# A graph layer on one core: the root ahead of the weights, minima behind the node tiles, zeros shared with ScalarE, and another order of VectorE's last steps

## The chip, the cores and the metric

The kernel runs on one core of a Trainium2 chip. The metric is the device time of one execution, in microseconds (us). Engines are named TensorE (PE in rows), VectorE (DVE), ScalarE (ACT), GpSimd (POOL) and SyncE (SP). They run side by side and wait for one another by semaphores.

## The reference

One layer of a message-passing network over 3125 nodes of 160 numbers (64 scalars and 32 vectors of 3) and 53125 edges, sorted by their destination.

```python
h = maximum(layernorm(x), 0)
s, v = h[:, :64], h[:, 64:].reshape(n, 32, 3)
xs = s @ W1_s / 8;  xv = einsum('nmc,mk->nkc', v, W1_v) / sqrt(32)
w = silu(edge_embed @ fc_w1 + fc_b1) @ fc_w2 + fc_b2          # 192 weights for each edge
xs_e, xv_e = xs[src], xv[src]                                  # gathered rows
msg = [w_ss*xs_e*sh0, w_vv*sum_c(xv_e*sh1)/sqrt(3), w_sv*xs_e (x) sh1, w_vs*xv_e*sh0]
agg = segment_sum(msg, dst, n) / sqrt(0.5)
out_s = agg_s @ W2_s / sqrt(96) + s @ Wsc_s / 8                # and the same for out_v
out = x + h + [silu(out_s[:, :64]), out_v * silu(out_s[:, 64:96])]
```

## The kernel before

**Node stage.** The nodes are 25 tiles of 125, in 5 groups of 5. For each group VectorE takes statistics (L291) and aggregates them to mean and variance (L296), ScalarE takes the root (`std`, L258), VectorE the reciprocal (L302) and the product -mean x scale (`nmr`, L303), and then writes the five normalised tiles (L309). TensorE transposes each tile (L413, L414). ScalarE applies the maximum while it copies the result to `hT` (L245). TensorE multiplies it with the weights (L428, L429), two tiles behind the transposes, and ScalarE copies the products of two tiles at a time to `prod` (L250). SyncE stores them to `table` in HBM, in five parts of 6, 6, 6, 4 and 3 tiles (L200). A root is issued by ScalarE behind the third tile of the group before it: `if t % G == 2`. The first root stands behind the scalings of the weights (L237, L239), which wait for their loads.

Beside this, work for the edge stage is done. VectorE's `minima` (eight instructions on 104 partitions, L317 to L327) finds the lowest destination of each tile of 128 edges. It stands behind group 1. TensorE's multiplication L419 spreads the minima over the partitions ahead of the products of tile 18, and `windows` (L355) takes the destinations relative to them. The accumulator `agg`, 12548 columns, is cleared: 8192 columns by four transfers of 2048 from a tile of zeros (L193), the other 4356 by ScalarE behind the last products (L253). ScalarE fills `emb` with zeros at the start (L234). GpSimd gathers 24 "raw" tiles, input rows instead of table rows (L220). VectorE takes moments of two of the four groups of 6 raw tiles here (`raw_moments`), the rest in the edge stage.

**Barrier.** The node stage is a block of its own. All engines meet at its end, then each reads the number of passes (L493). There is one pass here.

**Edge stage.** The 416 tiles of 128 edges are 104 steps of 4 tiles, numbered q from 0. In each, GpSimd gathers the rows of the sources (L535), one instruction per tile. Every fourth step from 11 on has a raw tile as its last, which TensorE multiplies itself, so that 392 gathers are left. A slot for gathered rows is free when VectorE has multiplied the step four earlier. TensorE makes the edge weights (L811, L824), VectorE multiplies them with the rows (`products`: L640 and twice L645), TensorE sums over edges by selectors (`scatter`: L829, L830, L834), and VectorE adds the sums into `agg` at 4 windows (`add_windows`: L625 and L631, which make the selectors of a step two later, and four times L683). Step q of VectorE's program does the additions of step q - 2 first, and then the products of step q. Nodes whose edges are all in leave beside: ScalarE copies their sums (L550), TensorE multiplies them (L859 to L866), ScalarE applies silu (L560, L561), VectorE multiplies by the gates (`gated`, L702), adds the input (`with_input` L695, `residual` L708), and SyncE stores the tile.

**The end.** The last step, 103, goes tile by tile: `last_products(j)` (L657, L661), `last_scatter(j)`, `last_add(j)` (L690). Its first three tiles are gathered, the fourth is the raw one. TensorE's order at the end is the weights of step 103, the sums of step 102, its own part of the last node tile, the last scatters 0 and 1, node tile 23, the last scatters 2 and 3, and the sums of node tile 24.

## Time and profile before

| | us |
|---|---|
| median of 3 runs | 546.01 (545.75 to 546.27) |
| the profiled execution | 545.95 |
| its span | 544.3 |
| GpSimd busy | 397.7 (73%) |
| TensorE busy | 475.8 (87%) |
| VectorE busy | 354.1 (65%) |
| ScalarE busy | 202.1 (37%) |
| mean granted TensorE clock | 0.936 of full |

The page divides the span by what ended last. 65% of that chain is the gathers of L535 and 22% is "issue", time in which an engine waited for nothing that the profile shows. TensorE's 87% includes the modelled ends of pipelined matmuls, so it is not an engine at its peak. A row of the timeline gives the start, the duration, the engine, the line and the operation, what it writes and reads, how many are merged in it, and in brackets the idle time ahead of it with what ended it.

### The profile page before, as it was taken

Reading aid. Unit: us, or ns where it says so; the run is one execution under the profiler, and the core shown is the slowest. Engines: PE = TensorE matmul, PEld = TensorE weight load, DVE = VectorE, ACT = ScalarE, POOL = GpSimd, SP = SyncE. Lnnn points to the kernel's source line nnn. Section 1 sums busy time; section 2 is a strip of 40 time slices with the busy share of each in tenths; the row PEclk is TensorE's granted clock in tenths of the full one; section 3 lists DMA queues with packets and bytes.
Section 4 is the critical chain, followed back from the end, with each engine's and each line's share of the span. In section 5 each row is a group of like instructions: output and inputs, shape, how many; then the busy total and the mean of one; then the engine's idle time right before and its main releaser. Section 6 shows DMA issues by size and latency. Waiting matters only on the chain.

```text
span 544.3 us, 16081 instructions
## 1 busy us (share of the span) xinstructions
PE 475.8 (87%) x5423; PEld 354.8 (65%) x5423; DVE 354.1 (65%) x1234; ACT 202.1 (37%) x412; POOL 397.7 (73%) x429
## 2 busy tenths in 40 slices
PE   6848779899898998999898999899898998998995
PEld 6745556667665765767575676567575765765675
DVE  7865565665676676567656766675576677676754
ACT  4564422343343333343333434343333334243331
POOL 7737777777777777777777777777777777777770
PEclk9888798899899899899997999899899899998996
DMA  9982222223222222222222222222222222222221
GB/s 223 395 265 72 70 71 71 67 66 81 77 76 67 76 73 69 74 77 76 65 73 77 66 77 77 76 65 74 77 76 67 77 77 69 72 75 75 66 75 30
DMA packets 35375, 48.06 MB, mean 88 GB/s; under 512 B 9749, under 2 KB 27956, under 8 KB 34844
## 3 DMA queue, kind: packets, MB, share of 16 engines
q0 software_dynamic: 19968, 34.11, 23.2%
q1 hardware_dynamic: 14977, 13.65, 8.4%
q8 instruction: 9, 0.15, 0.1%
q10 hardware_dynamic: 410, 0.07, 0.1%
q14 instruction: 11, 0.08, 0.0%
HBM read 39.60 MB, written 4.00 MB: 80 GB/s over the span
## 4 chain that ended last, share of the span: by engine, by line
POOL 65%; issue 22%; PE 4%; DVE 4%; DMA 3%; ACT 0%; ACTq 0%; DVEq 0%; SPq 0%
POOL gath L535 65%; DMA table<-prod 1%; DMA gath<-table,src_sb 1%; DMA w_v_in<-wscv 1%; PE ps L428 1%; PE ps L429 1%; DVE stats L291 1%; DVE z_sb L309 1%; DVE P L645 1%; PE ps L824 0%; PE ps L413 0%; PE ps L834 0%; PE ps L866 0%; PE ps L414 0%; ACTq L230 0%
## 5 line engine op out<-in xcount | busy, mean ns | idle before, releaser
L535 POOL DMA_INDIRECT gath<-table,src_sb x392 | 371.6, 948 | 125.9 <-issue 118.8
L834 PE MATMUL ps<-S,P 128*64 128x24 f32 x2496 | 170.7, 220 | 0.0
L824 PE MATMUL ps<-fc_sb,hid 128*128 128x384 f32 x416 | 164.9, 522 | 0.0
L829 PE MATMUL ps<-S,P 128*64 128x36 f32 x832 | 119.2, 237 | 49.3 <-DVE agg L683 48.3
L834 PEld LDWEIGHTS ps<-S,P 128*64 128x64 f32 x2496 | 159.5, 142 | 0.0
L829 PEld LDWEIGHTS ps<-S,P 128*64 128x64 f32 x832 | 82.3, 139 | 113.5 <-DVE agg L683 72.6
L640 DVE TENSOR_TENSOR P<-ps,gath 128x512 f32<-128x512 f32 x103 | 71.2, 692 | 125.5 <-PE ps L824 63.7
L568 ACT ACTIVATE hid<-ps,fb_sb 128x256 f32<-128x256 f32 x104 | 49.2, 473 | 185.7 <-PE ps L811 128.8
L830 PE MATMUL ps<-S,P 128*64 128x12 f32 x832 | 108.9, 209 | 0.0
L645 DVE TENSOR_TENSOR P<-ps,gath 128x384 f32<-128x384 f32 x206 | 104.3, 548 | 0.0
L824 PEld LDWEIGHTS ps<-fc_sb,hid 128*128 128x128 f32 x416 | 81.3, 206 | 34.4 <-issue 6.7
L683 DVE TENSOR_TENSOR agg<-ps,agg 128x48 f32 x412 | 84.5, 205 | 27.4 <-DVE agg L683 0.3
L583 ACT COPY ps<-fb_sb 128x768 f32<-128x768 f32 x104 | 83.9, 806 | 8.7 <-DVE P L645 8.5
L830 PEld LDWEIGHTS ps<-S,P 128*64 128x64 f32 x832 | 84.4, 142 | 0.0
L811 PE MATMUL ps<-emb,fc_sb 128*128 128x256 f32 x208 | 76.2, 449 | 0.0
L550 ACT COPY aggT<-agg 128x500 f32 (+1 forms) x24 | 26.9, 1119 | 40.4 <-DVE agg L683 40.4
L631 DVE TENSOR_TENSOR S<-M,sh_sb 128x192 f32<-128x192 f32 x104 | 37.3, 358 | 0.9
L560 ACT ACTIVATE gates<-ps 125x32 f32<-125x32 f32 x25 | 4.9, 197 | 84.1 <-PE ps L866 78.4
L811 PEld LDWEIGHTS ps<-emb,fc_sb 128*128 128x128 f32 x208 | 33.0, 198 | 4.2 <-issue 1.2
L625 DVE TENSOR_TENSOR M<-iota,dstrel 128x48 f32<-128x48 f32 x104 | 21.6, 208 | 15.6 <-issue 8.1
L220 POOL DMA_INDIRECT raw<-x,src_sb x24 | 22.8, 952 | 7.2 <-issue 7.2
L866 PE MATMUL ps<-wo_v,aggT 96*125 96x32 f32 x144 | 18.4, 264 | 0.0
(118 smaller groups left out, 351.9 us busy)
## 6 DMA issues: line engine op xcount, KB each, us to landing
gath<-table,src_sb POOLq DMA_INDIRECT x392, 2.5
agg<-zeros SPq DMA_DIRECT2D x4, 1024.0 KB, 16.9
out<-res SPq DMA_DIRECT2D x24, 78.1 KB
x_sb<-x SPq DMA_DIRECT2D x5, 350.0 KB
emb<-emb_t SPq DMA_DIRECT2D x104, 16.0 KB
table<-prod SPq DMA_DIRECT2D x3, 420.0 KB
sh_sb<-sh_t SPq DMA_DIRECT2D x1, 840.0 KB
raw<-x,src_sb POOLq DMA_INDIRECT x24, 7.3
```

The source lines that it names most:

```text
L535: nc.gpsimd.indirect_dma_start(gath[:, u, j, :], None, table, bass.IndirectOffsetOnAxis(ap=src_sb[:, t:t + 1], axis=0)).then_inc(arrived, 16)
L568: ins = nc.scalar.activation(hid[:, u % 2, :, :].rearrange("p g e -> p (g e)"), hid_ps, ACT.Silu, bias=fb1_sb[:, 0:1])
L583: nc.scalar.copy(w_ps(u)[:, :, 0:WN], fb2_sb[:, :].unsqueeze(1).broadcast_to([128, QT, WN])).then_inc(p_seed, 1)
L631: nc.vector.tensor_tensor(S[:, u % 2, :, :, :], M[:, :, :].unsqueeze(3).broadcast_to([128, QT, WIN, 4]), sh_sb[:, bass.ds(q * QT, QT), :]. ...
L640: nc.vector.tensor_tensor(pu[:, :, 0:128].rearrange("p j (a m) -> p j a m", a=2), w[:, :, 0:128].rearrange("p j (a m) -> p j a m", a=2), g ...
L645: ins = nc.vector.tensor_tensor(pu[:, :, 128:PC].rearrange("p j (c a m) -> p j c a m", c=NC, a=2)[:, :, :, a, :], w[:, :, lo:lo + V0].unsq ...
L683: nc.vector.tensor_tensor(a, out_ps(q)[:, j, :, :].rearrange("p n c -> p (n c)"), a, ALU.add).then_inc(p_agg, 1)
L811: ins = nc.tensor.matmul(hid_ps, fc1_sb[:, :], emb[:, u, :], start=True, stop=True)
L824: ins = nc.tensor.matmul(w_ps(u)[:, 2 * g:2 * g + 2, 0:WN], hid[:, u % 2, g, :], fc2_sb[:, :, :], start=False, stop=True, skip_group_check ...
L829: nc.tensor.matmul(oj[0:64, :, 0:3], pj[:, 64:128], sj[:, :, 1:4], start=True, stop=True)
L830: nc.tensor.matmul(oj[0:64, :, 3], pj[:, 0:64], sj[:, :, 0], start=True, stop=True)
L834: ins = nc.tensor.matmul(oj[64:128, :, c:4:3 - c], pj[:, lo:lo + 64], sj[:, :, 0:2 + c:1 + c], start=(c == 0), stop=(c == NC - 1), skip_gr ...
```

## The change

In the node stage:

- The first root is issued ahead of the scalings of the weights (`table_weights`).
- The product `nmr` goes. The tiles are normalised as (x - mean) x scale instead of x x scale + nmr.
- `minima` and the multiplication for it stand behind all the tiles.
- Two transfers of zeros are left. ScalarE clears four parts of 1024 columns behind tiles 2, 6, 11 and 16, and 4356 columns behind the last products as before. The fill of `emb` stands behind that.
- One raw group of four is taken in the node stage, and three in the edge stage.

At the end:

- VectorE adds the sums of step 101, and takes the inputs of the last two tiles, ahead of the products of step 102.
- The raw tile of step 103 is multiplied and summed first, and the first of the last additions stands between the products.
- The residual of node tile 22 stands behind the last additions.

```diff
-ZEROS, ZERO_DMA = 2048, 8192
+ZEROS, ZERO_DMA, ZERO_PART = 2048, 4096, 1024
+CLEARS = (2, 6, 11, 16)
-HEAD_RAW = 2
+HEAD_RAW = 1
 (ScalarE)
-                nc.scalar.copy(emb[:, :, :], zero[:, 0:1].unsqueeze(2).broadcast_to([128, SLOTS, 2 * TE]))
...
                 std(0)
+                table_weights()
                 for t in range(NN):
                     h_columns(t)
+                    if t in CLEARS:
+                        lo = ZERO_DMA + ZERO_PART * CLEARS.index(t)
+                        clear(lo, lo + ZERO_PART)
                     if t % G == 2 and t // G + 1 < NG:
                         std(t // G + 1)
...
-                clear(ZERO_DMA, (N + WIN) * AC)
+                clear(ZERO_DMA + ZERO_PART * len(CLEARS), (N + WIN) * AC)
+                nc.scalar.copy(emb[:, :, :], zero[:, 0:1].unsqueeze(2).broadcast_to([128, SLOTS, 2 * TE])).then_inc(s_cact, 1)
 (VectorE)
-                    link(nc.vector.reciprocal(rstd[:, sl], rstd[:, sl]))
-                    nc.vector.scalar_tensor_tensor(nmr[:, sl], meanvar[:, sl, 0], -1.0, rstd[:, sl],
-                                                   ALU.mult, ALU.mult).then_inc(s_rstd, 1)
+                    nc.vector.reciprocal(rstd[:, sl], rstd[:, sl]).then_inc(s_rstd, 1)
...
-                        nc.vector.tensor_scalar(z_sb[:, t, :], x_sb[:, t, :], rstd[:, t:t + 1], nmr[:, t:t + 1],
-                                                ALU.mult, ALU.add).then_inc(s_z, 1)
+                        nc.vector.tensor_scalar(z_sb[:, t, :], x_sb[:, t, :], meanvar[:, t, 0:1], rstd[:, t:t + 1],
+                                                ALU.subtract, ALU.mult).then_inc(s_z, 1)
...
-                    if g == 1:
-                        minima()
-                raw_moments(0)
+                minima()
+                for g in range(HEAD_RAW):
+                    raw_moments(g)
                 windows()
-                raw_moments(1)
 (VectorE, edge stage)
                     def step(i, u, tile=None):
                         q = i * SLOTS + u
+                        if isinstance(i, int) and q == NQ - 1:
+                            return last(tile)
...
+                        if isinstance(i, int) and q == NQ - 2:
+                            cols = columns(q - 1)
+                            add_windows(q - 1, u + 1, cols)
+                            with_input(NN - 2)
+                            with_input(NN - 1)
                         products(i, q, u)
...
                     def last(tile):
-                        residual(tile)
+                        last_products(QT - 1)
                         last_products(0)
-                        with_input(NN - 2)
-                        last_products(1)
-                        with_input(NN - 1)
                         cols, rest = columns(NQ - 2), columns(NQ - 1)
                         dve.wait_ge(n_cols, NN - 1)
                         add_windows(NQ - 2, SLOTS - 2, cols, more=False)
+                        last_products(1)
+                        last_add(0, rest[QT - 1])
                         last_products(2)
-                        last_products(3)
-                        for j in range(QT):
-                            last_add(j, rest[j])
+                        for k in range(1, QT):
+                            last_add(k, rest[k - 1])
+                        residual(tile)
```

`last_scatter` and `last_ps` count in the new order (k), and the tile that k stands for is (3 + k) mod 4.

On ScalarE, at the start of the node stage, these rows stand in the kernel before:

```order
L232 ACTIVATE root<-eps 125x1
L234 COPY emb<-zero 128x1024
L237 ACTIVATE w_s<-w_s 64x160
L239 ACTIVATE w_tab<-w_v_in,own_c 96x32 x3
L258 ACTIVATE rstd<-meanvar,eps 125x5
L245 ACTIVATE hT<-ps 96x250 x3
L258 ACTIVATE rstd<-meanvar,eps 125x5
```

And these in the changed one:

```order
L232 ACTIVATE root<-eps 125x1
L259 ACTIVATE rstd<-meanvar,eps 125x5
L238 ACTIVATE w_s<-w_s 64x160
L240 ACTIVATE w_tab<-w_v_in,own_c 96x32 x3
L246 ACTIVATE hT<-ps 96x250 x3
L254 COPY agg<-zero 128x1024
L259 ACTIVATE rstd<-meanvar,eps 125x5
```

The first root moved ahead of the scalings, the fill of `emb` left this place, and a clear of `agg` stands between the third tile and the next root.

On VectorE, at the end of the edge stage, from the products of step 102 on, the kernel before has:

```order
L640 TENSOR_TENSOR P<-ps,gath 128x4x128
L645 TENSOR_TENSOR P<-ps,gath 128x4x3x32 x2
L702 TENSOR_TENSOR res<-ps,gates 125x3x32
L668 TENSOR_LOAD base_i
L625 TENSOR_TENSOR M<-iota,dstrel 128x48
L683 ISA
L683 TENSOR_TENSOR agg<-ps,agg 128x48
L631 TENSOR_TENSOR S<-M,sh_sb 128x192
```

The changed kernel has, from the third addition of step 101's sums on (`ISA` is a wait):

```order
L685 ISA
L685 TENSOR_TENSOR agg<-ps,agg 128x48
L685 ISA
L685 TENSOR_TENSOR agg<-ps,agg 128x48
L697 SCALAR_TENSOR_TENSOR xh<-z_sb,x_sb 125x160 x2
L642 TENSOR_TENSOR P<-ps,gath 128x4x128
L647 TENSOR_TENSOR P<-ps,gath 128x4x3x32 x2
L704 TENSOR_TENSOR res<-ps,gates 125x3x32
L659 TENSOR_TENSOR P<-ps,gath 128x128
L663 TENSOR_TENSOR P<-ps,gath 128x192
```

The additions of step 101 and the two inputs moved from behind the products of step 102 to ahead of them, and the raw tile's products follow at once.

## Rows read from the trace of the kernel before

**Rows 1.** The page's groups of instructions: busy and mean | idle before.
```profile
L535 POOL DMA_INDIRECT gath<-table,src_sb x392 | 371.6, 948 | 125.9 <-issue 118.8
```

**Rows 2.** Timeline of GpSimd in the edge stage: first and last gather.
```profile
40.89 0.96 POOL L535 DMA_INDIRECT gath<-table,src_sb  x1 [6.79 <-DMA table<-prod]
...
530.62 0.95 POOL L535 DMA_INDIRECT gath<-table,src_sb  x1 [0.30 <-issue]
```

**Rows 3.** The chain of waits, 0 to 42 us: start, length, what.
```profile
28.38 0.70 PE ps L419 x2
...
33.05 0.30 ACT prod L250
...
35.16 5.08 DMA table<-prod
```

**Rows 4.** Timeline of VectorE, node stage and the first instruction behind it.
```profile
7.23 0.44 DVE L296 BATCH_NORM_AGGREGATE meanvar<-stats 125x2 f32<-125x6 f32 x5
8.57 0.17 DVE L303 SCALAR_TENSOR_TENSOR nmr<-meanvar,rstd 125x5 f32<-125x5 f32 x1
13.47 1.51 DVE L309 TENSOR_SCALAR z_sb<-x_sb,rstd,nmr 125x160 f32<-125x160 f32 x5
15.26 0.65 DVE L317 TENSOR_REDUCE dmax<-dq 104x4 f32<-104x512 int32 x1
...
17.78 1.22 DVE L291 BATCH_NORM_STATS2 stats<-x_sb 125x6 f32<-125x160 f32 x5
...
27.44 1.73 DVE L309 TENSOR_SCALAR z_sb<-x_sb,rstd,nmr 125x160 f32<-125x160 f32 x5
...
37.59 0.13 DVE L350 COPY raw_mean<-raw_mv 128x6 f32<-128x6 f32 x1
40.37 0.38 DVE L614 TENSOR_SCALAR dstrel<-dstrel 128x416 f32<-128x416 f32 x1 [2.66 <-PEq L180]
```

**Rows 5.** Timeline of ScalarE, node stage.
```profile
4.73 1.03 ACT L234 COPY emb<-zero 128x1024 f32<-128x1024 f32 x1
...
8.03 0.29 ACT L258 ACTIVATE rstd<-meanvar,eps 125x5 f32<-125x5 f32 x1
...
15.92 0.29 ACT L258 ACTIVATE rstd<-meanvar,eps 125x5 f32<-125x5 f32 x1
...
33.23 3.82 ACT L253 COPY agg<-zero 128x4356 f32<-128x4356 f32 x1
```

**Rows 6.** Timeline of TensorE: the first transpose of two tiles in succession.
```profile
29.36 0.27 PE L413 MATMUL ps<-ident,z_sb 125*64 125x125 f32 x1
...
30.01 0.27 PE L413 MATMUL ps<-ident,z_sb 125*64 125x125 f32 x1
```

**Rows 7.** Timeline of GpSimd, its last instruction in the node stage.
```profile
33.16 0.95 POOL L220 DMA_INDIRECT raw<-x,src_sb  x1 [0.30 <-issue]
```

**Rows 8.** Three stretches: busy us (instructions) by engine, granted clock, DMA share, GB/s.
```profile
17.20:20.62 3.42, 1.03 (x10) 0.88 (x9) 3.34 (x14) 0.93 (x3) 2.54 (x3) 1.00 1.01 394
20.62:24.04 3.42, 3.42 (x19) 3.30 (x18) 3.03 (x17) 1.73 (x5) 2.77 (x3) 0.50 1.02 393
...
36.00:38.00 2.00, 0.00 (x0) 0.00 (x0) 0.43 (x4) 1.45 (x3) 0.00 (x0) 0.92 1.04 292
```

**Rows 9.** Timeline of VectorE, the end.
```profile
529.37 0.69 DVE L640 TENSOR_TENSOR P<-ps,gath 128x512 f32<-128x512 f32 x1 [1.72 <-DMA gath<-table,src_sb]
...
531.07 0.20 DVE L625 TENSOR_TENSOR M<-iota,dstrel 128x48 f32<-128x48 f32 x1
...
537.31 0.21 DVE L690 TENSOR_TENSOR agg<-ps,agg 128x48 f32 x1 [0.20 <-PE ps L834]
```

**Rows 10.** Timeline of TensorE, the end.
```profile
528.83 0.51 PE L834 MATMUL ps<-S,P 128*64 128x24 f32 x6
...
531.04 0.25 PE L829 MATMUL ps<-S,P 128*64 128x36 f32 x1 [0.21 <-DVE P L645]
...
536.64 0.49 PE L834 MATMUL ps<-S,P 128*64 128x24 f32 x3
```

More of the change, by code:

```diff
@@ L33 @@
 EPS = 1e-5
-ZEROS, ZERO_DMA = 2048, 8192
+ZEROS, ZERO_DMA, ZERO_PART = 2048, 4096, 1024
 WARM_NODES = 17
-MINB_AT = 20
 PC = 320
@@ L124, in build @@
         rstd = sbt("rstd", [NTN, NN])
-        nmr = sbt("nmr", [NTN, NN])
         w_v_in = sbt("w_v_in", [VD, 2, V0])
@@ L232, in _, with table_weights @@
                 nc.scalar.activation(root[:, :], eps[0:NTN, :], ACT.Sqrt)
-                nc.scalar.copy(emb[:, :, :], zero[:, 0:1].unsqueeze(2).broadcast_to([128, SLOTS, 2 * TE]))
-                act.wait_ge(s_own, 2)
-                act.wait_ge(s_wn, 16 * len(node_loads))
-                nc.scalar.activation(w_s[0:S0, :], w_s[0:S0, :], ACT.Copy, scale=S0 ** -0.5)
-                for comp in range(NC):
-                    ins = nc.scalar.activation(w_tab[:, V0 * comp:V0 * (comp + 1)], w_v_in[:, 0, :], ACT.Copy,
-                                               scale=own_c[:, comp:comp + 1])
-                ins.then_inc(s_scaled, 1)
+                def table_weights():
+                    act.wait_ge(s_own, 2)
+                    act.wait_ge(s_wn, 16 * len(node_loads))
+                    nc.scalar.activation(w_s[0:S0, :], w_s[0:S0, :], ACT.Copy, scale=S0 ** -0.5)
+                    for comp in range(NC):
+                        ins = nc.scalar.activation(w_tab[:, V0 * comp:V0 * (comp + 1)], w_v_in[:, 0, :], ACT.Copy,
+                                                   scale=own_c[:, comp:comp + 1])
+                    ins.then_inc(s_scaled, 1)
                 def h_columns(t):
@@ L297, in mean_and_variance, with scale @@
                     ins.then_inc(s_stat, 1)
-                def scale_and_bias(g):
+                def scale(g):
                     sl = slice(g * G, g * G + G)
                     dve.wait_ge(s_std, g + 1)
-                    link(nc.vector.reciprocal(rstd[:, sl], rstd[:, sl]))
-                    nc.vector.scalar_tensor_tensor(nmr[:, sl], meanvar[:, sl, 0], -1.0, rstd[:, sl],
-                                                   ALU.mult, ALU.mult).then_inc(s_rstd, 1)
+                    nc.vector.reciprocal(rstd[:, sl], rstd[:, sl]).then_inc(s_rstd, 1)
                     dve.wait_ge(s_rstd, g + 1)
@@ L379, in _ @@
                 mean_and_variance(0)
-                scale_and_bias(0)
+                scale(0)
                 normalised(0)
@@ L386, in _ @@
                         tile_stats(g + 1)
-                    scale_and_bias(g)
+                    scale(g)
                     normalised(g)
@@ L415, in _ @@
                                             ident[0:NTN, 0:NTN]).then_inc(s_hT, 1)
-                    if t == MINB_AT:
-                        pe.wait_ge(s_ones, 1)
-                        pe.wait_ge(s_mm, 1)
-                        nc.tensor.matmul(minb_ps, ones[:, :], diag.rearrange("p q t -> p (q t)"),
-                                         start=True, stop=True).then_inc(s_minb, 1)
                     if t >= 2:
@@ L430, in _ @@
                                          start=True, stop=True).then_inc(s_prod, 1)
+                pe.wait_ge(s_ones, 1)
+                pe.wait_ge(s_mm, 1)
+                nc.tensor.matmul(minb_ps, ones[:, :], diag.rearrange("p q t -> p (q t)"),
+                                 start=True, stop=True).then_inc(s_minb, 1)
                 nc.tensor.transpose(most_ps, most[:, :], ident[0:NQ, 0:NQ]).then_inc(s_row, 1)
@@ L746, in step @@
                             add_windows(q - 2, u, cols)
-                        if isinstance(i, int) and q == NQ - 1:
-                            return last(tile)
+                        if isinstance(i, int) and q == NQ - 2:
[3 more added lines that the diff above has]
+                            with_input(NN - 1)
                         products(i, q, u)
```

28 lines of the change are left out of this document (14 added, 14 removed).

## The prediction, made before the changed kernel ran

> **What bounds the kernel now.** I read the page's groups first, then GpSimd's timeline, then the chain of waits. The 392 gathers of the edge stage are GpSimd's, and their group shows 125.9 us of idle time, of which 118.8 is its own issue gap [rows 1]. That leaves 7.1 us of true waiting, and 6.79 of it is the one wait ahead of the first gather [rows 2]. So from 40.89 to 530.62 us GpSimd never waits for TensorE, VectorE or ScalarE, and nothing in that stretch can be shortened by other engines. The profiled time of 544.3 us of span (545.95 with what lies around it, 0.06 under the median of 546.01) is three pieces: 40.89 until the first gather starts, 489.7 of gathers, and 13.7 from the start of the last gather to the end. The change touches the first and the last. It leaves the number of gathers alone.
>
> The first gather has two things ahead of it, and they are nearly tied. The chain goes by the last store of the table: last copy of products until 33.35 (33.05 + 0.30), its second store issued 35.16, landed 40.24 (5.08 later), gather 0.65 after that [rows 2, 3]. But VectorE ends the node stage at 37.72 (37.59 + 0.13), and its first instruction of the edge stage starts at 40.37, having waited for the barrier [rows 4]. I read the 0.65 us behind the landing, where 0.30 is the usual gap, as a sign that GpSimd too came through that barrier late. So both must get earlier, and I keep the distance from VectorE's end to the first gather, 40.89 - 37.72 = 3.17 us.
>
> **The node stage, part by part.** Call X the end of the last copy of products by ScalarE: 33.35 now.
>
> Root first, no second operand. The first group's moments end at 7.67 on VectorE (7.23 + 0.44) [rows 4], the root starts at 8.03, because four scalings of weights stand ahead of it [rows 5]. Behind the change it can start at 7.69: 0.34 gained. The scalings move behind it and end near 8.95, before the first transposed tile needs ScalarE. The product of mean and scale goes, an instruction of 0.17 and its gap, 0.20 per group [rows 4]. With two groups of it, normalising of group 1 starts at 13.47 - 0.34 - 0.40 = 12.73. The normalisation itself keeps its form and length.
>
> Minima behind the tiles. They hold VectorE from 15.26 to 17.78, 2.52 us [rows 4], and TensorE starves meanwhile. What is late next? Not VectorE: a group without minima and product takes it 3.1 us (statistics 1.1, being the 1.22 of the row less the overlap with the next, reciprocal 0.2, five tiles 1.45, aggregation 0.35). Not TensorE, at 0.65 per tile (29.36 to 30.01) or 3.3 per group [rows 6]. It is ScalarE, since the root of group g+2 stands behind the third tile of group g+1. Today from the start of group 1's normalisation (13.47) to the root at 15.92 are 2.45 us [rows 4, 5]. Each of the four clears of 1024 columns is the same operation as the fill of emb, 1.03 us [rows 5], of which I count 0.95 (the next one overlaps its end). 0.22 of it falls into a wait of ScalarE for TensorE, so the root comes 2.45 + 0.73 = 3.18 after the tiles start, and the next tiles 0.54 later (root 0.32, reciprocal 0.22): a period of 3.72 us. Three periods from 12.73: group 4 starts at 23.9, against 27.44 now.
>
> From there to X are 33.35 - 27.44 = 5.91 us today, with the multiplication for the minima, 0.70, in the middle, which goes behind [rows 3, 4]. So X = 23.9 + 5.91 - 0.70 = 29.1, 4.25 earlier. Bounds of this: TensorE's 3.3 per group instead of 3.72 gives X = 27.8; all of each clear on the path (3.95 per group) and 1.9 more for a stretch at the low clock gives X = 31.7.
>
> Behind X. The clear of 4356 columns stays, 3.82 [rows 5]. New between it and the root for the raw tiles is the fill of emb, +0.95; one root and one pair of VectorE instructions go, -0.19. VectorE now ends 37.72 - 33.35 = 4.37 after X, then 5.13 after X: 34.2. VectorE's own work does not end it: tiles done at 25.5, minima 2.5, moments 1.9, windows 1.0, rest 1.2, near 32.1. GpSimd does nearly: its raw gathers, untouched, end at 34.11 (33.16 + 0.95) [rows 7]. First gather: 34.2 + 3.17 = 37.4, **3.5 us earlier**. GpSimd's 34.11 is the floor, so no more than 3.6 can come of it, and with X = 31.7 it is 0.9.
>
> Zeros. The transfers run at a DMA share of about 1 until 38 us [rows 8], which is what makes the last store take 5.08. Two of the four 1 MB transfers go. At the 394 GB/s of the row at 17.20 their 2.1 MB (twice 128 x 2048 x 4 bytes) are 5.3 us of queue, so the last store lands near 35, ahead of the 36.9 at which VectorE passes the barrier (34.2 + 40.37 - 37.72). I cost it at nothing because ScalarE's clears cover it. If that were wrong, see the fourth rival.
>
> Raw groups. One more group of moments (6 statistics, 6 aggregations, 1.9 us) falls into the edge stage's first steps. GpSimd is released by VectorE's products four steps ahead and never waited, so: 0.
>
> **The tail.** Now, in VectorE's order: step 102 of 0 to 103 multiplies at 529.37, when the gather lands, after 1.72 us of waiting [rows 9]. The addition of step 101's sums follows at 531.07 and ends at 532.37, then the inputs of two tiles, 0.5 us. After the change these 1.8 us stand ahead of the multiplication. The idea needs step 101's sums to be ready while VectorE waits. They are not: TensorE ends them at 529.34 (528.83 + 0.51) [rows 10], the very moment the gather lands. So the additions start at 529.5, end at 530.8, inputs until 531.3, and the multiplication starts 1.9 us late. TensorE is what waits for it: its scatter of step 102 starts at 531.04 now [rows 10], at 532.95 then. From 531.04 to the end of the last scatter, 537.13, are 6.1 us [rows 10], of which I read 0.3 as waits for VectorE and 0.5 as the low clock; the other 5.3 (scatter 1.5, own part 0.5, two last scatters 0.8, node tile 1.4, two last scatters 1.1) are TensorE's own and end at 538.2. The last addition can start 0.15 later, 538.4, against 537.31 now [rows 9]: +1.1. If the last two scatters run at 1.2 GHz, as their like does now from 536.04 on, +1.5. I take **+1.3**. Raw tile first and the additions laid between are worth nothing by themselves, because TensorE is the later one. The residual moved behind the additions falls into VectorE's wait for the last tile's gates: 0, and its store still leaves ahead of the last tile's. Bounds: 0 (if a scatter ends earlier than this trace shows) to +2.9 (second rival).
>
> Sum: -3.5 + 1.3 = -2.2, from 546.0 to 543.8 us.
>
> **Clock.** While the minima hold VectorE, in the stretch from 17.20 to 20.62, TensorE was busy 1.03 of 3.42 us, and the next stretch was granted 0.50, 1.2 GHz [rows 8]. The minima made that gap, so I expect the node stage to keep 2.4 GHz. The tail gets a new gap, 530.8 to 532.95. The Trainium skill, "TensorE: Matmul & The Clock Gate", section "Part 1: The HAM clock gate", says that the clock follows how busy TensorE has been recently and that the observation runs free of the program. By that rule the node stage wins and the tail can lose; the trace agrees on the first place. It gives the second rival a chance, and the sum stays as it is without it.
>
> **Rivals.**
> 1. Forecast, 543.8, own range 542.9 to 544.9: 58%.
> 2. The new gap brings the tail to 1.2 GHz three microseconds earlier. Six tile scatters then cost 0.45 instead of 0.35 each, own part and node tile about 1 us more together: +1.6 to the tail, 545.4. For: [rows 8]. Against: the gap is 2.1 us, and that stretch had 2.4 idle. 17%.
> 3. No loss in the tail: step 101's scatter ends half a microsecond or more before the gather lands, or TensorE's tail work overlaps better. Then -3.5 alone, 542.5: 12%.
> 4. The change doesn't do what it says at the head: the last store is not freed by fewer zeros and lands at 40.2 still, because 640-byte rows and raw gathers fill the queues anyway. Head 0, tail +1.3: 547.3, 5%. Against: 2 MB less ahead of it.
> 5. The other side: ScalarE becomes the path. If each clear costs its full 0.95 and pushes root, reciprocal and tiles, and TensorE thereby idles into 1.2 GHz again in two groups, X moves to 33 or later; with 0.76 more behind X and 1.3 in the tail the sum is X - 32.6 + 1.3 (first gather X + 8.3 against 40.89): 546.4 at X = 31.7, 547.7 at X = 33.0. The point from which it decides: X later than 31.3 makes the head's gain smaller than the tail's loss. For: ScalarE has the longest period in my walk. Against: part of each clear falls into a wait it has anyway. 8%.
>
> Less than 0.2% (1.1 us) can't be told from no change here. Faster takes 1 and 3, 70%; no change takes 2, 17%, and a little of 5, 18%; slower takes 4 and most of 5, 12%. Range: 542.4 to 545.6, which leaves out 4 and 5 and a little beside.
>
> **What would show it.** First gather at 37.4 (37.0 to 38.5). No TensorE wait of over 1 us between groups 1 and 4, and no half clock near 20 us. Roots of groups 2 to 4 about 3.7 apart, VectorE waiting for ScalarE ahead of each reciprocal. Last copy of products near 29. Two engines, ScalarE's chain and GpSimd, at the barrier together at 34. DMA share falling before 33. In the tail the multiplication of step 102 about 1.9 later behind its gather's landing than now, a TensorE wait of 2 us ahead of that scatter, and last gather to end near 15.0 instead of 13.7. I am wrong if a gather in the middle waits, if the first gather stays behind a landing, or if the tail gets shorter.

## The result: slower, where faster was forecast

The changed kernel takes 548.27 us (median of 10 runs, 547.09 to 549.23), the kernel before 546.39 us beside it (10 runs, 545.55 to 547.13). The ratio is 1.0035, with an interval of 1.0024 to 1.0046: slower by 0.35%, or 1.9 us. The forecast was 543.8 us. The profiled execution took 548.27 us too, with a span of 546.5, against 544.3 before.

The two profiled executions, cut into the three pieces of the prediction (us):

| | first gather starts | gathers, first start to last | last gather's start to the end | span |
|---|---|---|---|---|
| before | 40.89 | 489.73 | 13.65 | 544.3 |
| after | 39.85 | 489.50 | 17.10 | 546.5 |

The head (all ahead of the first gather) gained 1.0, not 3.5. The tail (behind the last gather's start) lost 3.4, not 1.3. The middle is untouched. First the page of the changed kernel: its span, the granted clock in 40 slices, the group of the gathers (to be read beside [rows 1]) and the landing of the raw gathers.

```profile
span 546.5 us, 16078 instructions
...
PEclk9969799799799989989999899899899998998995
...
L537 POOL DMA_INDIRECT gath<-table,src_sb x392 | 371.3, 947 | 124.4 <-issue 123.8
...
raw<-x,src_sb POOLq DMA_INDIRECT x24, 3.8
```

GpSimd's idle time in the gathers is 124.4 us against 125.9, and all but 0.6 of it now reads "issue". That does not say that nothing was waited for: the wait ahead of the first gather is in it, without a name, as the next rows show. The raw gathers land 3.8 us after their issue (median); before it was 7.3. The last of them, on which the experiments turn, takes 3.8 from its start to its landing; before it was 5.2.

The node stage, ScalarE's timeline after the change (start, length, and in brackets the idle time before it and what ended that), for [rows 5]:

```profile
7.05 0.30 ACT L259 ACTIVATE rstd<-meanvar,eps 125x5 f32<-125x5 f32 x1 [2.23 <-DVE meanvar L302]
...
22.65 0.30 ACT L259 ACTIVATE rstd<-meanvar,eps 125x5 f32<-125x5 f32 x1
...
27.56 0.73 ACT L251 COPY prod<-ps 125x320 f32<-125x320 f32 x2 [0.39 <-PE ps L427]
28.18 3.82 ACT L254 COPY agg<-zero 128x4356 f32<-128x4356 f32 x1
31.91 1.05 ACT L280 COPY emb<-zero 128x1024 f32<-128x1024 f32 x1
```

VectorE's timeline, for [rows 4]:

```profile
22.98 0.19 DVE L308 RECIPROCAL rstd<-rstd 125x5 f32<-125x5 f32 x1 [1.62 <-ACT rstd L259]
23.20 1.53 DVE L313 TENSOR_SCALAR z_sb<-x_sb,meanvar,rstd 125x160 f32<-125x160 f32 x5
...
33.29 0.13 DVE L354 COPY raw_mean<-raw_mv 128x6 f32<-128x6 f32 x1
39.33 0.38 DVE L616 TENSOR_SCALAR dstrel<-dstrel 128x416 f32<-128x416 f32 x1 [5.91 <-PEq L180]
```

GpSimd's, for [rows 7] and [rows 2]:

```profile
33.58 0.95 POOL L220 DMA_INDIRECT raw<-x,src_sb  x1 [0.30 <-issue]
39.85 0.95 POOL L537 DMA_INDIRECT gath<-table,src_sb  x1 [5.33 <-issue]
```

Every engine's own node work did what was forecast. The last normalisation starts at 23.20 (before 27.44), the last copy of products ends at 28.29 (before 33.35), VectorE ends at 33.42 (before 37.72), and the last gather of GpSimd's own ends at 34.53. Then nobody works: VectorE waits 5.91 us for the barrier (line 180 is where the engines meet), GpSimd's next gather comes 5.33 us after its last. 4.3 us won on VectorE bought 1.0. The last store of the table landed at 34.80, near the 35 of the forecast, against 40.24 before, and did not hold the first gather either.

Stretches of 1 us and one of 4 us: length, busy us (instructions) of TensorE, its weight loads, VectorE, ScalarE and GpSimd, granted clock, DMA share, GB/s. After:

```profile
19.00:23.00 4.00, 3.86 (x33) 3.47 (x32) 2.02 (x12) 3.68 (x12) 2.97 (x4) 1.00 1.02 391
...
33.00:34.00 1.00, 0.00 (x0) 0.00 (x0) 0.24 (x2) 0.15 (x1) 0.69 (x2) 0.50 0.42 131
...
36.00:37.00 1.00, 0.00 (x0) 0.00 (x0) 0.00 (x0) 0.00 (x0) 0.00 (x0) 0.50 0.22 24
37.00:38.00 1.00, 0.00 (x0) 0.00 (x0) 0.00 (x0) 0.00 (x0) 0.00 (x0) 0.50 0.00 0
```

Before:

```profile
37.00:38.00 1.00, 0.00 (x0) 0.00 (x0) 0.43 (x4) 0.45 (x3) 0.00 (x0) 0.84 0.86 268
38.00:39.00 1.00, 0.00 (x0) 0.00 (x0) 0.00 (x0) 0.00 (x0) 0.00 (x0) 0.50 0.37 111
```

The queues run empty a good microsecond earlier than before, and the first gather is 1.0 earlier; the experiments show that the two hang together. Between 37 and 38.4 us nothing at all is to be seen in the changed kernel. The clock was 1.00 through the stretch around 20 us that had 0.50 before [rows 8].

The tail, VectorE's timeline after, for [rows 9]:

```profile
528.44 0.21 DVE L627 TENSOR_TENSOR M<-iota,dstrel 128x48 f32<-128x48 f32 x1 [1.68 <-PE ps L841]
...
529.76 0.55 DVE L697 SCALAR_TENSOR_TENSOR xh<-z_sb,x_sb 125x160 f32<-125x160 f32 x2
530.23 0.68 DVE L642 TENSOR_TENSOR P<-ps,gath 128x512 f32<-128x512 f32 x1
...
539.48 0.21 DVE L692 TENSOR_TENSOR agg<-ps,agg 128x48 f32 x1 [0.43 <-PE ps L841]
```

TensorE's, for [rows 10]:

```profile
531.89 0.25 PE L836 MATMUL ps<-S,P 128*64 128x36 f32 x1 [2.00 <-DVE P L647]
...
535.20 0.73 PE L866 MATMUL ps<-w_s,hTt 96*125 96x96 f32 x2
...
536.57 1.36 PE L873 MATMUL ps<-wo_v,aggT 96*125 96x32 f32 x6
```

Two stretches of it, columns as above:

```profile
530.80:534.30 3.50, 2.41 (x54) 2.28 (x54) 2.54 (x10) 0.46 (x2) 0.00 (x0) 1.00 0.09 23
534.34:537.70 3.36, 3.36 (x28) 3.31 (x24) 1.66 (x8) 0.00 (x0) 0.00 (x0) 0.50 0.00 0
```

VectorE used to wait for a gather ahead of the multiplication of step 102 (1.72 us [rows 9]). Now it waits the same time, 1.68, for TensorE's sums of step 101, and the additions and the inputs come behind that. The multiplication starts 0.88 us after the last gather's start; before it was 1.25 ahead of it (529.37 against 530.62). Of these 2.1 us only 1.5 are the change's: by the trace's records of landings the gathers of step 102 have landed 0.64 ahead of the last gather's start here and 1.28 before. TensorE waits 2.00 us, and from 534.34 on it has 1.2 GHz. From the start of this scatter to the last addition's start are 7.59 us, 6.27 before. With the scatter's own 2.1 us of lateness (2.54 after the last gather's start, 0.42 before) that is the 3.4.

The fall of the clock at 534.34 stands behind the wait, but it need not come of it. These stretches of the changed kernel run from fall to rise and from rise to fall:

```profile
459.25:462.67 3.42, 3.42 (x8) 1.70 (x7) 1.26 (x7) 1.43 (x3) 2.72 (x3) 0.50 0.38 107
462.67:496.80 34.13, 30.78 (x399) 23.23 (x399) 23.57 (x76) 12.40 (x25) 25.65 (x28) 1.00 0.26 70
496.80:500.21 3.41, 3.41 (x8) 1.59 (x6) 1.29 (x6) 1.43 (x3) 2.75 (x3) 0.50 0.40 109
500.21:534.34 34.13, 30.88 (x410) 23.39 (x410) 22.46 (x78) 11.12 (x23) 22.78 (x25) 1.00 0.24 64
```

In the edge stage the granted clock falls again and again, and from 196.43 us on each fall comes 37.55 us behind the one before it; 534.34 is the next of this row. The kernel before has its last fall, at 536.04, 37.55 behind the one at 498.49 too. Counted from the last gather's start the falls lie close together, 4.99 here and 5.41 before. What differs is the work that is left then: 5.1 us to the start of the last addition here, 1.3 before.

### The profile page after: what moved, and what is told of

It reads as the page before. It is cut to its first block and busy times, and to the rows that moved or that the text cites. A ratio compares the mean times of both kernels' runs of the same rounds, so it can differ in the third digit from the quotient of the medians.

```text
span 546.5 us, 16078 instructions
## 1 busy us (share of the span) xinstructions
PE 475.8 (87%) x5423; PEld 353.0 (65%) x5423; DVE 353.2 (65%) x1229; ACT 205.2 (38%) x416; POOL 397.9 (73%) x429
## 3 DMA queue, kind: packets, MB, share of 16 engines
q0 software_dynamic: 19968, 34.11, 23.1%
## 5 line engine op out<-in xcount | busy, mean ns | idle before, releaser
L537 POOL DMA_INDIRECT gath<-table,src_sb x392 | 371.3, 947 | 124.4 <-issue 123.8
L841 PE MATMUL ps<-S,P 128*64 128x24 f32 x2496 | 169.0, 219 | 0.0
L818 PE MATMUL ps<-emb,fc_sb 128*128 128x256 f32 x208 | 77.3, 456 | 0.0
```

Source lines behind the costliest of these rows:

```text
L537: nc.gpsimd.indirect_dma_start(gath[:, u, j, :], None, table, bass.IndirectOffsetOnAxis(ap=src_sb[:, t:t + 1], axis=0)).then_inc(arrived, 16)
L818: ins = nc.tensor.matmul(hid_ps, fc1_sb[:, :], emb[:, u, :], start=True, stop=True)
L841: ins = nc.tensor.matmul(oj[64:128, :, c:4:3 - c], pj[:, lo:lo + 64], sj[:, :, 0:2 + c:1 + c], start=(c == 0), stop=(c == NC - 1), skip_gr ...
```

## The experiments

Each kernel was timed beside the kernel before on the same chip. The table has ratios of medians, and from the one profiled execution the landing of the last raw gather (the last signal of its transfers, from the trace's records of landings), the first gather behind the barrier (in e5 it is a raw one; its first gather from the table starts at 43.31), the tail (last gather's start to the end), and how long after the last gather's start the granted clock fell for good.

| kernel | ratio, interval | last raw landing | first gather | tail | clock falls |
|---|---|---|---|---|---|
| before | 1 | 38.39 | 40.89 | 13.65 | +5.41 |
| after | 1.0035, 1.0024 to 1.0046 | 37.35 | 39.85 | 17.10 | +4.99 |
| e1_old_tail | 0.9983, 0.9971 to 0.9996 | 37.04 | 39.54 | 15.99 | +4.37 |
| e2_new_tail_only | 1.0054, 1.0035 to 1.0074 | 39.33 | 41.84 | 16.80 | +4.74 |
| e3_inputs_up | 0.9972, 0.9960 to 0.9984 | 37.05 | 39.56 | 14.40 | +7.80 |
| e4_fill_gap | 1.0014, 0.9999 to 1.0029 | 37.03 | 39.53 | 15.18 | +8.12 |
| e5_six_late | 1.0100, 1.0079 to 1.0122 | 31.51 | 35.82 | 18.95 | +6.47 |
| e6_zeros_dma | 1.0005, 0.9993 to 1.0017 | 39.08 | 41.58 | 16.44 | +4.58 |
| e8_minima_back | 0.9986, 0.9973 to 0.9998 | 38.52 | 41.02 | 14.56 | +8.15 |
| e9_new_end | 0.9963, 0.9950 to 0.9975 | 37.15 | 39.65 | 14.51 | +9.50 |
| e10_end_and_start | 0.9956, 0.9942 to 0.9970 | 36.46 | 38.97 | 14.08 | +9.55 |
| e11_sums_up | 1.0010, 0.9997 to 1.0024 | 37.04 | 39.54 | 14.51 | +8.65 |

### The two halves: e1_old_tail and e2_new_tail_only

e1 is the changed kernel with the old end (the order of `step` and `last`, and of the last scatters); e2 is the kernel before with the new end.

```diff
 # e1, against the changed kernel
-                        if isinstance(i, int) and q == NQ - 2:
-                            cols = columns(q - 1)
-                            add_windows(q - 1, u + 1, cols)
-                            with_input(NN - 2)
-                            with_input(NN - 1)
...
-                        last_products(QT - 1)
+                        residual(tile)
                         last_products(0)
+                        with_input(NN - 2)
+                        last_products(1)
+                        with_input(NN - 1)
```

> The changed kernel's node stage with the old order of VectorE and TensorE at the end. Theory (the head gains 1.0 us, the tail loses 3.4 us): first gather near 39.9, start of the last gather to the end 13.7 as before, so 545.3 us, 1.0 under the kernel before. Rival (the whole change loses by something in the middle, such as the third raw group in the edge stage or a different phase of TensorE's clock, and the tail is only where it shows): the end stays near 17 us behind the last gather, 548 us.

> The old node stage with the new order at the end. Theory: first gather at 40.9, last gather to the end 17.1 instead of 13.7, so near 549.6 us, 3 or more above before. Rival (it is the two parts together that lose): 546 to 547 us.

Measured: e1 545.47 us (12 runs) against 546.65, a gain of 0.17%; e2 549.50 us (6 runs), a loss of 0.54%. The new end costs as much on the old node stage (0.54%) as on the new (1.0035 less 0.9983, 0.52%, some 2.8 us). The new node stage is a small gain, about 1 us, and the new end more than eats it. The halves add up: there is no third cost in their meeting.

In its profile e1 has a tail of 15.99 us, though 13.7 was expected and its end is the old one. Its clock fell at 533.15, 4.37 after the last gather's start, with no late scatter behind it:

```profile
495.60:499.02 3.42, 3.42 (x12) 2.38 (x11) 1.69 (x8) 1.65 (x4) 2.51 (x4) 0.50 0.34 88
499.02:533.15 34.13, 31.82 (x418) 23.75 (x417) 22.38 (x78) 11.16 (x24) 23.39 (x25) 1.00 0.28 68
533.15:536.56 3.41, 3.41 (x30) 3.30 (x27) 1.97 (x10) 0.28 (x2) 0.00 (x0) 0.50 0.02 7
```

That is again 37.55 us behind the fall before. So profiles with an early fall (after, e1, e2, e6) and with a late one (e3, e4, e8, e11; see the table) are not to be compared with each other; the kernel before lies between. From the start of step 102's scatter to the last addition's start e1 takes 7.76 us, and e8, with the same end and a late fall, 6.27. Among the early ones the new end's tail is 17.10 and 16.80 (after, e2), the old end's 15.99 and 16.44 (e1, e6): 0.4 to 1.1 us. Among the late ones e4, the new end with a filled gap, has 15.18, and e8, the old end, 14.56: 0.6. The medians say 2.8, over all executions, so the larger part is probably that the early fall comes more often with the new end. That is an argument from single profiles, and the share isn't shown.

e2's head is that of the kernel before, and its first gather came at 41.84, not 40.89. Its table had landed at 40.20, as before (40.24), so the 0.65 us between that landing and the first gather [rows 2, 3] were no fixed distance: here they are 1.64. The first gather of the old node stage thus varies by about 1 us from one execution to the next; in six kernels with the new node stage as it is (after, e1, e3, e4, e9, e11) it lies within 39.53 to 39.85.

### What sets the first gather: e5_six_late, e6_zeros_dma, e8_minima_back

e5 keeps the changed kernel, and issues the last group of six raw gathers behind the barrier, in the edge stage:

```diff
-                for r in range(NR):
+                for r in range(NR - RG):
...
                 def _(pool):
+                    for r in range(NR - RG, NR):
+                        t = (RAW_FROM + r) * SLOTS * QT + SLOTS * QT - 1
+                        nc.gpsimd.indirect_dma_start(
+                            raw[:, r, :], None, x,
+                            bass.IndirectOffsetOnAxis(ap=src_sb[:, t:t + 1], axis=0)).then_inc(s_raw[r // RG], 16)
                     pool.wait_ge(s_tabw, TABLE_IN)
```

> The changed kernel with the last group of raw gathers (6 of 24) issued by GpSimd in the edge stage, ahead of its first table gather, instead of in the node stage. Theory A (GpSimd comes last to the barrier, because it comes only some 1.4 us after the transfers of its last raw gather have ended): the barrier then is VectorE's, which ends near 33.7, so GpSimd's first instruction of the edge stage starts near 35.3 instead of 39.9; its six gathers take 7.5 us, the first table gather is near 42.8, total near 551. Theory B (the wait at the barrier belongs to ScalarE's and VectorE's chain, as in the prediction, with a longer way through the barrier): GpSimd starts at 39.9 as before and the total is 555 to 556.

Measured: 552.73 us (4 runs) against 547.24. Its timelines of VectorE and GpSimd behind the last work of the node stage:

```profile
33.93 0.13 DVE L354 COPY raw_mean<-raw_mv 128x6 f32<-128x6 f32 x1
...
35.28 0.38 DVE L621 TENSOR_SCALAR dstrel<-dstrel 128x416 f32<-128x416 f32 x1 [1.22 <-PEq L180]
...
35.82 0.94 POOL L530 DMA_INDIRECT raw<-x,src_sb  x1 [9.17 <-issue]
```

VectorE's wait for the barrier shrinks from 5.91 to 1.22 us, and GpSimd issues again at 35.82, 4.0 earlier. So the barrier was late because of those six gathers, and for nothing else. As a version it loses: the six cost 6 x 1.25 = 7.5 us ahead of the gathers of the edge stage, and win 4.0 (3.5 net; measured 0.65% over the changed kernel, 3.6 us). Its one profile is 5.0 us over that of the changed kernel, because there the tail is longer too (18.95), and why is open.

Which part of those gathers does the barrier wait for? GpSimd is done with issuing at 34.5. The table answers: the first gather starts 2.50 us after the last raw landing (2.50 or 2.51) in eleven of the twelve rows; the twelfth is e5, where VectorE came last. GpSimd's program doesn't ask for this wait: behind its gathers it waits only for the zeros, which landed at 25.4 (31.4 before). Nor does every engine wait so. In the kernel before, SyncE issued its last store of the table at 35.16, and was through the barrier while that store was under way (it landed at 40.24):

```profile
40.20 1.98 SPq L504 DMA_DIRECT2D emb<-emb_t  x4
```

So what is shown is shown for GpSimd's gathers.

e6 is e1 with the zeros given back to the queues. e8 is e1 with the minima back behind group 1.

```diff
 # e6
-ZEROS, ZERO_DMA, ZERO_PART = 2048, 4096, 1024
+ZEROS, ZERO_DMA, ZERO_PART = 2048, 8192, 1024
...
-CLEARS = (2, 6, 11, 16)
+CLEARS = ()
 # e8
-                minima()
+                    if g == 1:
+                        minima()
```

> The changed node stage with the old end, but with all four transfers of zeros (8192 columns) and no clears by ScalarE between the tiles; compared with the kernel that has the new node stage and the old end (545.5). Theory A (the barrier waits for the last raw gather to land): the queues are full again when it is issued, it lands 1 to 2 us later, first gather near 40.9 and 546.5, though ScalarE's tiles end earlier than with the clears. Theory B (ScalarE's chain sets the barrier): without 3.8 us of clears in it the first gather comes earlier, 545 or under.

> The changed node stage with the old end, but VectorE's minima stand behind group 1 again (the multiplication for them stays behind the tiles). Theory A (the barrier waits for the last raw gather to land): tiles and VectorE end some 2 to 3 us later, near 36, still ahead of the barrier at 38.1, so the time stays at 545.5. Theory B (the node stage's own chain sets it): 2 us more, 547.5.

Measured: e6 547.42 us (12 runs), 0.22% or 1.2 us above e1. All of e1's gain goes, although in e6 VectorE ended early (34.66); the two intervals (up to 0.9996, from 0.9993) just overlap. e8 546.34 us (12 runs), 0.9986 against e1's 0.9983. Here the first rows of GpSimd's edge stage in e6, and VectorE's end and GpSimd's start in e8:

```profile
33.18 0.95 POOL L220 DMA_INDIRECT raw<-x,src_sb  x1 [0.30 <-issue]
41.58 0.95 POOL L537 DMA_INDIRECT gath<-table,src_sb  x1 [7.46 <-issue]
```

```profile
37.84 0.13 DVE L354 COPY raw_mean<-raw_mv 128x6 f32<-128x6 f32 x1
...
41.02 0.95 POOL L538 DMA_INDIRECT gath<-table,src_sb  x1 [6.93 <-issue]
```

In e6 GpSimd issued its last raw gather 0.40 earlier than in the changed kernel and started the edge stage 1.73 later: its transfers lay in a queue with 2 MB more of zeros, and landed at 39.08. The place of the minima is worth nothing that can be measured; the intervals leave room for some 0.7 us. In e8's one profile the first gather is late (41.02), while the median is e1's; a single head is not to be trusted to better than about 1 us, the medians are.

### The tail: e3_inputs_up, e11_sums_up, e4_fill_gap

e3 is e1 with the inputs of the last two tiles alone ahead of the products of step 102, e11 is e1 with step 101's additions alone there:

```diff
 # e3
+                        if isinstance(i, int) and q == NQ - 2:
+                            with_input(NN - 2)
+                            with_input(NN - 1)
 # e11
+                        if isinstance(i, int) and q == NQ - 2:
+                            cols = columns(q - 1)
+                            add_windows(q - 1, u + 1, cols)
                         products(i, q, u)
```

> The new node stage with the old end, except that VectorE takes the inputs of the last two tiles ahead of the products of step 102, in its wait for the gather; step 101's sums stay behind. Theory (what costs is only that step 101's sums are not ready when the gather lands): the inputs fit into the 1.7 us wait, the products of step 102 start when the gather lands, and 0.5 us leave VectorE's row of work at the end, 0.2 to 0.5 us under the old end. Rival (any work moved ahead of the products delays them): 0.5 us above it.

> The new node stage with the old end, except that VectorE adds step 101's sums ahead of the products of step 102; inputs, raw tile and additions stay in the old order. Theory (this one move makes the scatter of step 102 late, by 1.4 us plus what TensorE's row behind it loses at the low clock): 1.5 to 2.5 us above the old end, 0.9983 + 0.0035 = 1.002. Rival (the loss came from the raw tile first and the addition between the products): like the old end, 0.998.

VectorE's timeline of e3, where the multiplication still waits for its gather:

```profile
526.25 0.55 DVE L697 SCALAR_TENSOR_TENSOR xh<-z_sb,x_sb 125x160 f32<-125x160 f32 x2
528.40 0.69 DVE L642 TENSOR_TENSOR P<-ps,gath 128x512 f32<-128x512 f32 x1 [1.60 <-DMA gath<-table,src_sb]
```

And of e11, where it waits for TensorE, and behind that for the additions:

```profile
528.86 0.21 DVE L627 TENSOR_TENSOR M<-iota,dstrel 128x48 f32<-128x48 f32 x1 [1.69 <-PE ps L839]
...
530.17 0.68 DVE L642 TENSOR_TENSOR P<-ps,gath 128x512 f32<-128x512 f32 x1
```

Measured: e3 545.01 us (7 runs), 0.11% or 0.6 us under e1, with intervals that overlap; e11 547.27 us (12 runs), 0.27% or 1.5 us over e1. The inputs need nothing that is late and fill the wait. The additions need sums that end shortly before the gather lands, or with it (529.34 and 529.37 in the kernel before). In e11 the sums end at 528.82, the gathers have landed at 529.59, and the additions hold the multiplication until 530.17: 0.58 us behind the landing, where e1 has 0.02. They fill a part of the wait and lengthen it by the rest.

The lengthening alone doesn't make the 1.5 us. In its profile e11 has a tail of 14.51, with a late fall, no longer than e8's 14.56 with the old end and a late fall. By the mean granted clock of each kernel's executions (0.933 over e11's 12, 0.936 over e1's 12) e11 had more time at 1.2 GHz, so a part of the 1.5 us is probably the clock.

e4 is the changed kernel with two matmuls of 384 columns, whose result nobody reads, in the new gap of TensorE:

```diff
+                    for _ in range(2):
+                        nc.tensor.matmul(ps[0:128, 1, 0:384], x_flat[:, 0:128], x_flat[:, 0:384], start=True, stop=True)
                     scatter(NQ - 2, 0)
```

> The changed kernel with two added multiplications of 384 columns on TensorE, into an unused bank, in its 2.0 us wait for the products of step 102; nothing else changes. Theory A (the wait brings the clock down to 1.2 GHz early, 2.1 us of the tail's loss is the later scatter and 1.3 us the clock): with the gap filled the clock stays at 2.4 GHz longer, 1 us under the changed kernel, 547.2. Theory B (the clock falls some 5 us behind the last large multiplications whatever stands in the gap): granted clock and time as in the changed kernel, or the fall comes about 1 us later, 0 to 0.5 us under it.

Measured: 547.30 us (12 runs), 1.0014 against 1.0035 of the changed kernel, 0.21% or 1.1 us better; the intervals (up to 1.0029, from 1.0024) overlap a little. TensorE's timeline and two stretches of it:

```profile
529.43 1.46 PE L906 MATMUL ps<-x_sb 125*128 125x384 f32 x4
531.59 0.25 PE L836 MATMUL ps<-S,P 128*64 128x36 f32 x1 [0.70 <-DVE P L647]
...
535.27 0.77 PE L873 MATMUL ps<-wo_v,aggT 96*125 96x32 f32 x6
```

```profile
533.70:537.10 3.40, 3.16 (x53) 2.96 (x52) 2.03 (x11) 0.31 (x2) 0.00 (x0) 1.00 0.00 0
537.12:540.50 3.38, 2.04 (x8) 1.90 (x8) 1.50 (x6) 0.31 (x2) 0.00 (x0) 0.50 0.16 47
```

The scatter is as late as in the changed kernel (2.59 after the last gather's start, against 2.54), yet the tail is 1.9 shorter: the node tile's last product takes 0.77 instead of 1.36, with the clock falling at 537.12 and not at 534.34 (8.12 after the last gather's start, against 4.99). This profile shows what the early fall costs, 2.1 us (from the scatter's start to the last addition's start 5.46 us, against 7.59). It doesn't show how often the filling prevents it: it is of an execution of 545.74 us, one of three near 545.7 with the highest mean clock of the twelve (0.940), and the other nine took 546.52 to 549.36.

All executions together speak for the filling. The mean granted clock of an execution is 0.932 on average over the changed kernel's 10 (0.929 to 0.936) and over e2's 6, and 0.936 over e4's 12 (0.930 to 0.940), as much as over e1's 12. One stretch like that from 496.80 to 500.21 lowers the mean of such an execution by 0.003 (an estimate, 3.41 x 0.5 / 546), so e4 has about one less. That the filling kept the clock is likely and not proved: e3, e8, e9 and e11 fill nothing, and in their profiles the clock fell late as well.

### Versions that gain: e9_new_end, e10_end_and_start

e9 is e1 with another end: inputs up as in e3, three last products ahead of step 102's additions, the first last addition between, the residual behind, the hT copy of ScalarE ahead of its wait, and the third last scatter ahead of the node tile. e10 is e9 with ScalarE filling `zeros`, so that GpSimd starts its raw gathers earlier.

```diff
 # e9
-                        residual(tile)
-                        last_products(0)
-                        with_input(NN - 2)
-                        last_products(1)
-                        with_input(NN - 1)
+                        for j in range(3):
+                            last_products(j)
...
-                    node_tile(NN - 2)
                     last_scatter(2)
+                    node_tile(NN - 2)
 # e10
-                nc.gpsimd.memset(zeros[:, :], 0.0).then_inc(s_agg, 1)
...
+                nc.scalar.copy(zeros[:, :], zero[:, 0:1].broadcast_to([128, ZEROS])).then_inc(s_agg, 1)
```

> A new end on the changed node stage, meant to be faster: inputs taken in VectorE's wait ahead of the products of step 102 (step 101's sums behind them, as in the kernel before), three tiles of step 103 multiplied while ScalarE copies node tile 23's sums, the fourth between the last additions, residual of tile 22 behind them, TensorE's third last scatter ahead of node tile 23, and ScalarE's copy of the transposed tile ahead of its wait. Theory (in the kernel with only the inputs moved up VectorE is what the last addition waits for: 0.42 us for ScalarE's copies, 0.41 per addition, 0.24 for the residual): 0.7 us under that kernel, 544.3. Rival (TensorE is as late, since its row of work is the same): 545.0 as there.

> The kernel with the new end, and ScalarE fills the tile of zeros (2048 columns, 1.9 us, in its idle time ahead of the first root) instead of GpSimd. Theory (GpSimd's line of 24 raw gathers, their landing and the barrier is the whole head): its first raw gather starts when the sources' rows have landed, near 3.8 instead of 4.26, so barrier and first table gather come 0.4 us earlier, 0.9955 of the kernel before. Rival (the start of the raw gathers is not what counts; the transfers of zeros come later and the queue ends where it did): no change against the kernel with the new end, 0.9963.

Measured: e9 544.85 us (10 runs), ratio 0.9963, 0.5 us under e3 but within its interval. e10 544.52 us (5 runs) against 546.94, ratio 0.9956: faster than the kernel before by 2.4 us, and of all that ran the lowest ratio, though its interval holds e9's. GpSimd's timeline of e10:

```profile
3.70 1.10 POOL L219 DMA_INDIRECT raw<-x,src_sb  x1 [1.37 <-DMA src_sb<-src_t]
...
32.64 0.95 POOL L219 DMA_INDIRECT raw<-x,src_sb  x1 [0.30 <-issue]
38.97 0.95 POOL L537 DMA_INDIRECT gath<-table,src_sb  x1 [5.38 <-issue]
```

The raw gathers start 0.56 earlier (3.70 against 4.26), and the first gather comes 0.68 earlier than e9's. That is one profile of each, where the same node stage gave first gathers 0.3 us apart (six kernels) and 1.0 apart (before, e2), and the ratios' intervals overlap. So the earlier start is a likely gain and not a shown one.

## Why the prediction was wrong

Right, by its own steps. The end of the last products, 29.1 forecast, 28.29 measured. VectorE's end, 34.2 and 33.42. Group 4's normalisation at 23.9, measured 23.20, with roots at 7.05 and 22.65. No half clock near 20 us, so rival 5 did not come, and zeros at nothing on ScalarE's side. The table's last store near 35, 34.80. The DMA share fell at 33, the latest that was named. The middle: 489.5 us. In the tail a TensorE wait of 2 us, measured 2.00. The multiplication was to come 1.9 later behind its gather's landing and came 1.5 later; another 0.6 us is a later landing, so that its 2.1 against the last gather's start is partly chance.

**The step that failed is "GpSimd does nearly: its raw gathers, untouched, end at 34.11. First gather: 34.2 + 3.17 = 37.4."** It measured 39.85. The 34.11 was the end of an instruction that issues a gather, and I took it for GpSimd's arrival at the barrier. GpSimd is let through only when the gathers have landed: the first gather starts 2.50 us after the last landing, 38.39 before and 37.35 after. The 3.17 us from VectorE's end was not a distance at all, since VectorE was not the last one: before, it ended at 37.72 and the barrier opened at 39.46, 1.07 after the last raw landing. e6 shows that an earlier VectorE is worth nothing by itself: it ended at 34.66 there, and the first gather came at 41.58. The gain that there was came from the part that I costed at nothing, 2 MB less in the queues (e6: 1.2 us by the medians). It is a cousin of rival 4, "640-byte rows and raw gathers fill the queues anyway", but on GpSimd's gathers, not on the table's last store, which was freed as forecast. A hint was in the rows: VectorE's wait of 2.66 us for the barrier at 40.37 [rows 4], which no engine's work explained; in e5, where VectorE comes last, it is 1.22. I read past it. The prediction's own sign of being wrong, "if the first gather stays behind a landing", came true, with another landing than the one that was meant.

**The tail's term was too small: 1.3 us forecast, 3.4 in the profiles.** The lateness was about right; what failed is "the other 5.3 ... are TensorE's own", the stretch from the scatter of step 102 to the end of the last scatter, which stood for the usual clock. It measured 7.45 us, with 1.2 GHz from 534.34 on, 2.45 us after the scatter began (before 536.04, 5.00 after it began), where the forecast let only the last two scatters have it. With the late fall of e4 the same stretch took 5.27, so the term was right for one state of the clock and 2.2 us short for the other. The fall itself came hardly earlier than before (4.99 after the last gather's start, 5.41 before); the work came later and ran into it.

The rule cited with the forecast (the Trainium skill, "TensorE: Matmul & The Clock Gate", "Part 1: The HAM clock gate": the clock follows how busy the engine has lately been) is not decided by this fall: it stands behind the 2.00 us wait, but also in a row of falls 37.55 us apart, and e1 and e6 had theirs as early with the old end (4.37 and 4.58). e4's higher mean clock goes the way of the rule; e11's late fall behind a wait of 1.53 us doesn't. The nearest rival is rival 2, given 17%: "the new gap brings the tail to 1.2 GHz three microseconds earlier", priced at +1.6 in the tail and 545.4 in all. By medians the new end costs 2.8 us (e1 against after), near the bound of +2.9 that rival 2 set for the tail. Its size was right; its "three microseconds earlier" was not seen. The step of the additions costs 1.5 of it (e11, clock included), and the filling gives 1.1 back (e4); the two overlap and are no sum. The inputs, which gain 0.6 in e3, stand behind the additions in the changed kernel, and there they are 0.5 us more on the path.

With the head at -1.0 and the tail at its bound of +2.9 the sum would have been 547.9; measured 548.27. So the sign was lost in the head: even with the tail as measured, +3.4, a head of -3.5 would have left no loss.

Open: how the tail's loss divides exactly, since the clock fell 4.4 to 9.5 us after the last gather's start in the twelve profiles, and one profile of each kernel doesn't tell habit from chance (e1's profiled execution was 1.0 us over its own median and e6's 1.6, with an early fall, e4's 1.6 and e11's 1.4 under it, with a late one); what sets the moment of the fall; and whether e9 and e10 differ.

## What to carry to other kernels

GpSimd with gathers under way arrives at a barrier when they have landed, not when its last instruction ends (SyncE's store did not hold it so); where all wait and none works, read the DMA share before you give the barrier to the engine that computes last. Work laid into a wait gains only if its own inputs are there when the wait begins: the inputs of the tiles were, the sums of the step before were not, and with the additions ahead of it the multiplication came 0.6 us behind its gather's landing (e11), with the inputs behind them 1.5. Where TensorE makes the end, a delay can cost more than its length, because more of the work may fall behind the moment when the clock falls. And look where that moment lies before you compare the tails of two profiles: here it moved them by 1.5 to 2.1 us, with the same program behind it or nearly so.

## What was not expected of the hardware

- The first gather behind the barrier starts 2.50 us after the last landing of the same engine's earlier gathers, to 0.01 us in eleven kernels. Of this, 1.07 lie between the landing and the barrier's release in the trace, and 1.43 between that and the gather.
- The same gathers of 128 rows of 640 bytes land 7.3 us (before) and 6.4 us (e6) after issue beside four transfers of zeros, and 3.6 to 5.9 us beside two (after, e1, e3, e4, e9, e11; medians of the pages). The last of them, which sets the barrier, took 5.2 to 6.2 us beside four (before, e2, e6), and 3.5 to 3.9 beside two in those six kernels; but 5.4 in e8, beside two and with the table's stores issued later, so the zeros are not the only thing that counts.
- In the edge stage the granted clock fell again and again, in rows of falls 37.55 us apart, in all twelve profiles.
- In twelve kernels with nearly the same tail the clock fell between 4.37 and 9.55 us after the last gather's start. In five of them (before, after, e1, e2, e6) that was 37.55 us behind the fall before, in four (e3, e4, e8, e11) 40.96.
